# A graph layer on one core: x B made block by block while sorting, and its rows gathered in place of x's

## What is computed

```python
# x: 12500 x 128 fp32; src, dst: 200000 edges
h_self   = x @ W_lin + b_lin
messages = x[dst] @ W_msg + b_msg
msg_sum  = segment_sum(messages, src, 12500)
counts   = segment_sum(ones, src, 12500)
h_agg    = msg_sum / maximum(counts, 1)[:, None]
h   = concatenate([h_self, h_agg], axis=1) @ W_upd + b_upd
out = layernorm(x + relu(h), axis=-1)
```

## Time and profile before

| | |
|---|---|
| median of 3 runs | 1346.77 us (1344.6 to 1347.03) |
| the profiled execution | 1345.13 us |
| its span, first to last instruction | 1343.4 us |
| mean granted PE clock, share of full speed | 0.954 |
| busy: PE / DVE / ACT / POOL | 1188.4 / 980.0 / 680.3 / 633.6 us |
| loads of the windows, first and last issue | 252.5 and 327.4 us |
| loads of the first two routing tables, when the last bin is full | 416.67 us |
| first product of the main stage | 440.6 us |

### The profile page before, as it was taken

The page is one execution under the profiler, slowest core; times in us unless marked ns, Lnnn a source line. Parts: engine busy times, 40 slices in busy tenths (PEclk is TensorE's granted clock), DMA queues, the critical chain, the costliest instruction groups (busy, mean ns, idle before and its releaser), DMA issues.

```text
span 1343.4 us, 42226 instructions
## 1 busy us (share of the span) xinstructions
PE 1188.4 (88%) x16596; PEld 727.1 (54%) x16596; DVE 980.0 (73%) x2386; ACT 680.3 (51%) x978; POOL 633.6 (47%) x673
## 2 busy tenths in 40 slices
PE   2839799799783889999999999999999999999996
PEld 2838788799782334444444444444444444444443
DVE  7999989999994546666666666666666666666665
ACT  1313333111110556666666666666666666666664
POOL 2000000000000667767777776777777777767772
PEclk9969999789895889999999999999999999999998
DMA  7313333233003445555555555555555555555531
GB/s 109 104 54 119 129 111 111 72 107 101 6 2 122 115 110 158 156 153 158 158 158 155 156 151 141 142 142 146 141 152 157 157 157 158 157 153 159 157 89 43
DMA packets 124985, 168.86 MB, mean 126 GB/s; under 512 B 34771, under 2 KB 93952, under 8 KB 124716
## 3 DMA queue, kind: packets, MB, share of 16 engines
q1 hardware_dynamic: 92226, 101.17, 23.3%
q0 software_dynamic: 31280, 64.23, 20.3%
q10 hardware_dynamic: 1290, 0.78, 0.2%
HBM read 142.91 MB, written 23.21 MB: 124 GB/s over the span
## 4 chain that ended last, share of the span: by engine, by line
PE 65%; DVE 27%; issue 4%; ACT 2%; DMA 1%; POOL 1%; DVEq 0%; POOLq 0%; ACTq 0%
PE slot L1269 30%; PE acc L1283 21%; PE acc L1294 6%; DVE big L815 6%; DVE big L793 5%; DVE big L847 3%; PE slot L1319 2%; DVE big L840 2%; ACT big L578 2%; PE acc L1302 2%; DVE big L1005 1%; PE acc L1157 1%; PE slot L1310 1%; DVE big L800 1%; DVE big L806 1%
## 5 line engine op out<-in xcount | busy, mean ns | idle before, releaser
L578 ACT ACTIVATE big<-slot 128x768 bf16<-128x768 f32 x750 | 567.6, 809 | 308.4 <-PE slot L1269 308.4
L651 POOL DMA_INDIRECT big<-x,dst_at x500 | 481.6, 963 | 189.2 <-issue 73.3
L1269 PE MATMUL slot<-big 128*128 128x384 bf16 x2300 | 447.3, 329 | 23.0 <-ACT big L578 16.8
L946 DVE TENSOR_SCALAR big<-big,iota_k 128x512 bf16<-128x512 f16 x575 | 196.4, 371 | 279.9 <-PE slot L1269 276.3
L1269 PEld LDWEIGHTS slot<-big 128*128 128x128 bf16 x2300 | 190.2, 98 | 253.4 <-issue 129.1
L1283 PE MATMUL acc<-big 32*128 32x385 bf16 x6000 | 309.8, 325 | 0.0
L1283 PEld LDWEIGHTS acc<-big 32*128 32x128 bf16 x6000 | 124.8, 93 | 160.6 <-issue 110.3
L646 POOL MEMSET big<- 128x4 bf16 x6 | 0.3, 96 | 430.8 <-issue 430.8
L655 POOL DMA_INDIRECT big<-x,sp_i x150 | 144.6, 964 | 67.9 <-PE slot L1269 36.8
L956 DVE TENSOR_TENSOR big<-col_lo,iota_lo 128x512 bf16<-128x512 f16 x375 | 156.4, 417 | 0.0
L1294 PE MATMUL acc<-big 32*128 32x385 bf16 x2000 | 124.4, 323 | 6.8 <-DMA big<-x,dst_at 6.6
(11 more groups left out here) (143 smaller groups left out, 863.2 us busy)
## 6 DMA issues: line engine op xcount, KB each, us to landing
big<-rows SPq DMA_DIRECT2D x25, 1920.0 KB
x<-big SPq DMA_DIRECT2D x19, 480.0 KB, 2.9
big<-x,dst_at POOLq DMA_INDIRECT x500
big<-x SPq DMA_DIRECT2D x32, 192.0 KB, 2.5
big<-in_x SPq DMA_DIRECT2D x24, 256.0 KB
big<-base SPq DMA_DIRECT2D x24, 256.0 KB
out<-big SPq DMA_DIRECT2D x24, 256.0 KB
big<-in_x SPq DMA_DIRECT2D x19, 320.0 KB, 3.9
```

What stands on the lines that cost most here:

```text
L578: act.activation(xg[n % NX][:, :, 0:F3], slot[z % 2][:, :, 0:F3], ACT.Copy).then_inc(s["xg_ready"], 1)
L651: pool.indirect_dma_start(out=xg_d[:, c, 0:F3], out_offset=None, in_=x3_dram, in_offset=bass.IndirectOffsetOnAxis(ap=dst_at[:, q, c:c + 1] ...
L946: last = nc.vector.tensor_scalar(W[R_ % NW_][:, k, :].rearrange("p (c h n) -> p c h n", c=4, h=4), brow[q % NB].rearrange("p (h c n) -> p ...
L1269: ins = nc.tensor.matmul(slot[z % 2][:, j, 0:F3], W[R_ % NW_][:, k, (c % 4) * P:(c % 4 + 1) * P], xwin[:, win_at(c) + k, :], start=k == 0, ...
```

## The change

`x B` is made beside `x A` in the sorting stage, from the same transposed block, and it is `x B` that is split in three bf16 parts and stored as `x3`. So the gathered rows already are messages without their bias, and the main stage has no transpose and no product by B: DVE multiplies the sums by 1/count and adds base in one operation per 128 nodes. The blocks become 25 of 512 rows, so that both products fit in `slot[1]`. In the sorting loop PE's order becomes count_before(u+1), make_base(u), add_ranks(u), turn_x(u+1), fill_bins(u-1). `count_before` does both chunks in one product of 200 columns, 20 products instead of 40. SP waits for the transpose before it loads a block again, and stores base before x3. The `PACE` points go, and a gather waits for its tile alone. The layer, root and normalizing steps move to runs 7, 8 and 9.

```diff
-    XB, XJ = 20, 5
+    XB, XJ = 25, 4
...
+        r1_blk = pre.take(XJ * F, f32)
...
-        TURN, UPDATE, ROOT, LAYER, NORM = 5, 8, 10, 9, 11
+        LAYER, ROOT, NORM = 7, 8, 9
...
             def cast_hi(b):
-                act.wait_ge(x_loaded[b % 2], 16 * (b // 2 + 1))
+                act.wait_ge(s["base_made"], b + 1)
...
-                act.activation(x3_blk[b % 2][0:n, :, 0:F], x_blk[b % 2][0:n, :].rearrange("p (j f) -> p j f", f=F),
+                act.activation(x3_blk[b % 2][0:n, :, 0:F], slot[1][0:n, 1, :].rearrange("p (j f) -> p j f", f=F),
...
@@ ACT's sorting loop
-                if 0 < u < XB:
+                if u < XB:
                     cast_hi(u)
+                    take_base(u)
+                if u + 1 < XB:
+                    take_xT(u + 1)
                 if u < XB:
-                    take_xT(u)
                     cast_mid(u)
-                if u < XB:
-                    take_base(u)
...
@@ POOL, the gathers of a quad
                     for i, (kind, n) in enumerate(GATHERS):
-                        _, name, steps = PACE[i]
-                        if (q - 1) * PER_QUAD[name] + steps > 0:
-                            pool.wait_ge(s[name], (q - 1) * PER_QUAD[name] + steps)
                         if q > 0:
                             if kind == "chunk":
                                 pool.wait_ge(s["dma_added"], (q - 1) * ND + n // 2 + 1)
...
@@ DVE, split_1
                 dve.wait_ge(s["hi_cast"], b + 1)
-                dve.wait_ge(s["x_turned"], b + 1)
+                if b > 0:
+                    dve.wait_ge(s["lo_made"], b)
...
-                nc.vector.tensor_tensor(x3b, x3b, x3_blk[b % 2][0:n, :, 0:F], ALU.subtract).then_inc(s["r1_made"], 1)
+                nc.vector.tensor_tensor(r1_blk[0:n, :].rearrange("p (j f) -> p j f", f=F), slot[1][0:n, 1, :].rearrange("p (j f) -> p j f", f=F),
+                                        x3_blk[b % 2][0:n, :, 0:F], ALU.subtract).then_inc(s["r1_made"], 1)
...
@@ DVE, the end of a quad
-                    k = mark(nc.vector.reciprocal(cnt[:, 1, :], cnt[:, 0, :]))
-                    dve.wait_ge(s["sums_taken"], q + 1)
-                    after(k)
-                    nc.vector.tensor_tensor(S, S, bc(cnt[:, 1, :], F), ALU.mult).then_inc(s["S_ready"], 1)
+                    nc.vector.reciprocal(cnt[:, 1, :], cnt[:, 0, :]).then_inc(s["counts_turned"], 1)
...
-                    dve.wait_ge(s["h_made"], q + 1)
...
-                    nc.vector.tensor_tensor(Y, base4[q % 2], slot[z % 2][:, 0, :].rearrange("p (h f) -> p h f", f=F), ALU.add).then_inc(s["h_read"], 1)
-                    dve.wait_ge(s["h_read"], q + 1)
+                    for h in range(4):
+                        ins = nc.vector.scalar_tensor_tensor(out=Y[:, h, :], in0=S[:, h, :], scalar=cnt[:, 1, h:h + 1], in1=base4[q % 2][:, h, :], op0=ALU.mult, op1=ALU.add)
+                    ins.then_inc(s["S_read"], 1)
...
@@ PE, count_before
-                for k in range(2):
-                    for a in range(TP):
-                        for j in range(2):
-                            ins = nc.tensor.matmul(R_ps[u % 2][:, k * H:(k + 1) * H], tri16[0:EP, 0:EP], OH[u % 4][0:EP, k * TP + a, :, j],
+                of = OH[u % 4][0:EP, :, :, :].rearrange("p (k a) h j -> p k a h j", k=2)
+                for a in range(TP):
+                    for j in range(2):
+                        ins = nc.tensor.matmul(R_ps[u % 2].rearrange("p (k h) -> p k h", k=2), tri16[0:EP, 0:EP], of[:, :, a, :, j],
...
@@ PE, make_base
                 pe.wait_ge(s["xT_taken"], b + 1)
                 if b > 0:
                     pe.wait_ge(s["base_taken"], b)
+                    pe.wait_ge(s["hi_cast"], b)
+                    pe.wait_ge(s["r1_made"], b)
+                for k, w in ((1, B), (0, A)):
+                    for j in range(XJ):
+                        ins = nc.tensor.matmul(slot[1][0:n, k, j * F:(j + 1) * F], xT_blk[:, j * P:j * P + n], w, start=True, stop=True)
...
@@ PE's sorting loop
                 if u + 1 < U:
                     count_before(u + 1)
+                for k in range(NS - 1):
+                    if u == US * (k + 1) + 2:
+                        pe.wait_ge(s["lo_taken"], k + 1)
+                if u < XB:
+                    make_base(u)
                 add_ranks(u)
-                if u < XB:
-                    if u == US + 2:
-                        pe.wait_ge(s["lo_taken"], 1)
-                    turn_x(u)
-                    make_base(u)
+                if u + 1 < XB:
+                    turn_x(u + 1)
                 if u > 0:
                     fill_bins(u - 1)
...
@@ PE's main loop
-                        if q > 0 and r == TURN:
-                            turn(q - 1)
-                        if q > 0 and r == UPDATE:
-                            update(q - 1)
```

More of the change, by code:

```diff
@@ L275, in gnn_program @@
                 GATHERS += [("chunk", 2 * dma_pair_of(r)), ("chunk", 2 * dma_pair_of(r) + 1)]
[L277 to L303, removed]
         def xb_rows(b):
@@ L312, in bc @@
             return a.unsqueeze(2).to_broadcast([a.shape[0], a.shape[1], n])
-        turns = []
-        for q in range(Q + 1):
-            for r in range(RUNS):
-                if q < Q:
-                    turns += [("pair", q * STEPS + 2 * r), ("pair", q * STEPS + 2 * r + 1)]
-                if q > 0 and r == TURN:
-                    turns.append(("turn", q - 1))
-                if q > 0 and r == UPDATE:
-                    turns.append(("h", q - 1))
-        turn_of = {k: z for z, k in enumerate(turns)}
         block = ctx.enter_context(nc.Block())
@@ L530, in take_xT @@
                     act.wait_ge(s["base_made"], b)
-                act.activation(xT_blk, slot[0][:, :, :].rearrange("p a e -> p (a e)")[:, 0:XJ * P], ACT.Copy).then_inc(s["xT_taken"], 1)
+                act.activation(xT_blk, slot[0][:, 0, :], ACT.Copy).then_inc(s["xT_taken"], 1)
             def take_base(b):
@@ L537, in take_base @@
                 n = xb_rows(b)
[L538 removed]
+                act.activation(base_blk[b % 2][0:n, :], slot[1][0:n, 0, :], ACT.Copy).then_inc(s["base_taken"], 1)
             act.wait_ge(s["wT_made"], 1)
@@ L1209, in make_base @@
                 pe.wait_ge(s["xT_taken"], b + 1)
+                n = xb_rows(b)
                 if b > 0:
                     pe.wait_ge(s["base_taken"], b)
-                n = xb_rows(b)
-                for j in range(XJ):
-                    o = slot[1][0:n, j // 4, j % 4 * F:(j % 4 + 1) * F]
-                    ins = nc.tensor.matmul(o, xT_blk[:, j * P:j * P + n], A, start=True, stop=True)
+                    pe.wait_ge(s["hi_cast"], b)
[3 more added lines that the diff above has]
+                        ins = nc.tensor.matmul(slot[1][0:n, k, j * F:(j + 1) * F], xT_blk[:, j * P:j * P + n], w, start=True, stop=True)
                 ins.then_inc(s["base_made"], 1)
@@ L1303, in aggregate_spills @@
                     ins.then_inc(s["spilled"], 1)
-                def turn(q):
-                    z = turn_of[("turn", q)]
-                    slot_free(z)
-                    pe.wait_ge(s["S_ready"], q + 1)
-                    for h in range(4):
-                        ins = nc.tensor.transpose(slot[z % 2][:, 0, h * P:(h + 1) * P], S[:, h, :], ident[:, :])
-                    ins.then_inc(s["S_turned"], 1)
-                def update(q):
-                    z = turn_of[("h", q)]
-                    slot_free(z)
-                    pe.wait_ge(s["SX_taken"], q + 1)
-                    for h in range(4):
-                        o = slot[z % 2][:, 0, h * F:(h + 1) * F]
-                        ins = nc.tensor.matmul(o, SX[:, h, :], B, start=True, stop=True)
-                    ins.then_inc(s["h_made"], 1)
                 for q in range(Q + 1):
```

78 lines of the change are left out of this document (27 added, 51 removed).

## The result

The changed kernel takes 1300.72 us in the median of 4 runs (1298.47 to 1302.77), beside 1345.68 us for the kernel before on the same chip (4 runs, 1343.99 to 1347.03). The ratio is 0.9666, with a 95% interval of 0.9642 to 0.969. The forecast was 1296 us and the range 1285 to 1312. The total is 4.7 us off, but two of its terms were off by more, and in opposite directions.

The account below looks back on a forecast made before the run. PE was taken to bound the main stage (busy 195.19 of 200 us) and DVE the sorting stage. From the profiled 1345.1 us: -48.5 (PE), +0.5 (sorting), -1.2 (end) gave 1295.9, predicted as 1296 us; range 1285 to 1312.

Parts of the forecast that it names:

- What goes from PE: Main stage: transposes, product by B and a slot wait leave PE, 2.02 us a quad, 48.5 us over 24 quads.
- half comes back: Rival, main stage: half of PE's gain returns as waits for ACT's copies or the root, 1320 us; chance 0.06.
- Without `PACE` POOL keeps up, cost 0: Main stage gathers: at 1.257 us a step, 26 take 32.7 us of a 33.16 us quad, so nothing is lost.
- POOL just binds: Rival, main stage: from 1.275 us a step PE waits for gathers; at 1.30 us, 12 us lost, 1308; chance 0.12.
- the second rival: Main stage: gathers held by DVE's L946, one in three by up to 371 ns, step 1.38 us, 1355 us; chance 0.04.
- the rule on ports: Gathers: DVE in some modes blocks POOL's descriptors for a whole instruction; one L946 per gather would add 241 us.
- Nothing of PE's work depends on the points themselves: Main stage: without the points gathers start once their tile is free and POOL reaches them; removal counted as 0.
- Sorting +0.5: Sorting stage in all: splits +0.9 us and waits behind slabs -0.4 us, together 0.5 us longer.
- The splits and the pair: Sorting, DVE: 50 splits at 0.61 us replace 40 at 0.74, +0.9 us; a pair with a block takes 8.8 us.
- The waits behind the slabs: Sorting, DVE: waits of 4.2 us for transposes and 3.6 for ranks, nearly all behind slabs, change by only -0.4 us.
- The rival "better": First quad and sorting: the first quad's 6.6 us and most waits behind slabs go too, 1285 us; chance 0.10.
- The end: Behind the last quad: DVE's constants begin 0.73 us sooner, four 128-column operations follow, 1.2 us saved.

Follow-up runs that it names:

- the version with its nodes early: Changed kernel with DVE's node tables of two gathered pairs made one run earlier (runs 7, 9 instead of 8, 10): 1280.12 us, ratio 0.9537; 1604.04 us on a slower chip.
- with points: Changed kernel with the `PACE` points put back before the gathers: 1397.91 us, ratio 1.0398; on a slower chip 1487.53 us, ratio 0.9935.
- the new order alone: Kernel before with only the sorting loop's new PE order (base ahead of ranks, transposes a pair ahead), count unchanged: 1500.44 us, ratio 1.0023, on a slower chip.

## Why the prediction was right, and where it was not

**What goes from PE: right.** The 2.02 us a quad are there, and a little more. In the version in which POOL keeps up the quad lost 35.18 - 33.03 = 2.15 us. ACT's copies cost no more than before (16.5 us of waits against 16.2), and "half comes back" is out.

**"Without `PACE` POOL keeps up, cost 0": failed.** This is the step that was wrong. The step between gathers was 1.304 us and not 1.257. It had been read from the first quad, in which DVE has no quad to finish, and so no layer step and no normalizing in front of its tables. The margin of half a microsecond a quad was never there: the mean of all gathers before, 0.963 us, makes 26 steps of some 32.9 us, beside a quad of 33.16. The rival "POOL just binds" is what happened, down to its example: it named 1.30 us a step, a loss of 12 us and 1308 us. Against the forecast of 48.5 the loss was 48.5 - 33.7 = 14.8 us. Against the version with its nodes early it was (33.78 - 33.03) x 24 = 18 us, since PE's shorter order gives 3 us more than was forecast. The mechanism of the second rival was right too, a gather that is held by DVE's tables, but not by L946, the windows table it named (see the rule on ports), and it is not one in three by 371 ns. In most quads it is two in 26, by some 0.45 and 0.8 us, where three tables stand in a row.

**"Nothing of PE's work depends on the points themselves": incomplete.** Leaving them in would have cost 97 us. The forecast gave their removal no term of its own.

**Sorting +0.5: failed, -11.8.** The splits and the pair were right (8.75 us against 8.8; 25 pairs of 8.75 and 15 of 7.56 are 0.4 us more than 20 of 9.03 and 20 of 7.56). The 0.13 us that the working calls fixed is the difference between 640 and 512 columns; taken off 0.74 it gives the right 0.61 all the same (0.60 in the trace of the changed kernel). The waits behind the slabs had been counted as 4.2 + 3.6 = 7.8 us on DVE and nearly kept. The slabs became 2.9, 2.5 and 1.0 us cheaper instead. PE's gaps in the layouts, which none of the rows showed, became shorter too, 5.1 us in all instead of 13.2. The last slab, with 7.96 us of such gaps on the path, was left out of the working. The rival "better" named this (first quad and slabs, 1285), but with a first quad that gave nothing: its wait is 5.94 us, before 6.63.

```profile
461.91 0.83 PE L1234 MATMUL acc<-big 32*128 32x385 bf16 x8 [5.94 <-DMA big<-x,dst_at]
```

**The end: right**, -1.5 us against -1.2. On DVE's timeline the four operations of 128 columns take 1290.06 - 1288.89 = 1.17 us (1.18 said), and the relu's operation stands 4.9 us behind the start of the sums instead of 6.3.

```profile
1285.15 1.75 DVE L924 TENSOR_REDUCE big<-acc 128x512 f32<-128x1536 f32 x1
...
1288.89 1.14 DVE L948 SCALAR_TENSOR_TENSOR big<-big,cnt 128x128 f32<-128x128 f32 x4
1290.06 0.69 DVE L951 SCALAR_TENSOR_TENSOR big<-big 128x512 f32<-128x512 f32 x1
```

**The sum** was 1295.9 and the profiled execution 1298.5: +14.8 for POOL, -12.3 for sorting, -0.3 for the end, and 0.3 outside the span. The total was right by cancellation, which is luck: with the sorting stage as long as forecast the median would have been 1300.7 + 12.3 = 1313 us, just outside the range.

**The rule on ports.** Gathers of 1.40 and 1.74 us against 0.95 stand beside DVE's tables in the trace. The excess of 0.79 us is longer than the one windows table there (0.35 us), and near the two nodes tables that follow it (0.84 us in all). The Trainium skill, SBUF — State Buffer, section "Who interferes with whom", lets a DVE operation in a two-port mode block POOL's descriptors for its whole length, while one with two SBUF inputs contends with what POOL reads alone. The traces speak for the second: the nodes tables are made from two tables in SBUF, the windows table from one and a column of scalars. In five traces of the first kind of chip (before, the changed kernel twice, with nodes early, with points), 360 gathers have nothing but windows tables beside them on DVE, and 359 of these last 0.94 or 0.95 us like a gather beside an idle DVE (the other one 1.06). 146 have a single nodes table beside them, and 84 of these are over 1 us, up to 1.15. So a windows table alone does not hold a gather, and a nodes table alone does, by up to 0.2 us. Why two of them behind a windows table hold it for 0.45 to 0.8 us, and only when it begins at certain points of the train, stays open.

## What to carry to other kernels

- A queue that is 93% full, as POOL here, is no spare: take its step from a stretch in which all the other engines do all of their work, not from the first round, and list what stands beside its longest instances.
- Points that hold transfers back are for a queue that has time. When the consumer becomes faster, measure the kernel with and without them: here they would have cost 97 us on one kind of chip, and on the other the versions without them were the slow ones.
- When a stage is bound by one engine but starts or ends with a long run of tiny products on another, read the gaps in that run, and where they stand. Halving the products elsewhere gave some 10 us.

## What was not expected of the hardware

- The same program takes 1344 us on some chips and 1497 us on others. The granted clock is nearly the same over the span (0.954 on the first, 0.951 on the second with the new order alone). The difference is in the main stage. Late signals between engines are seen there, many of them where gathers begin freely, but they are not the whole of it. The changes have another sign there: the best version on the first kind (ratio 0.954) is a loss of 7% on the second.
- A gather on POOL is 0.95 us long, and up to 1.75 us when it begins beside three tables of DVE in a row. A windows table alone leaves it at 0.95 us.
- Gaps of up to 5.8 us in which PE waits for nothing shown, within 320 products of 25 columns. In kernels with the same sorting code they stand behind the same products each time.
